# Attention and gated experts on one core: other places for the small products of the period, and the first batch's first score tiles straight from SBUF

## The reference

```python
x = x + attention(layernorm(x), w_qkv, w_out, b_out)      # 16 heads of width 8
x = x + experts(layernorm(x), router_w, router_b, w1, w3, w2)   # 4 experts, the best 2 per token
# attention weights: s = (q k^T) / sqrt(8); t = s - max(s); stablemax3(t) / sum,
#   for t < 0: 1 / (1 - t (1 - t/2 (1 - t/3)))
# expert: (silu(x w1) * (x w3)) w2, weighted by the two normalised gates, all in float32
```

## Time and profile before

| | us |
|---|---|
| median of 3 runs (lowest, highest) | 1129.02 (1128.45, 1129.56) |
| the profiled execution | 1130.74 |
| its span, first to last instruction | 1129.0 |

### The profile page before, as it was taken

One profiled execution on the slowest core, in us unless ns is written; L12 is line 12 of the kernel. 1 busy time (PEld: TensorE's weight loads), 2 busy tenths in 40 slices (PEclk: granted clock), 3 DMA queues, 4 the chain that ended last, 5 costly groups with the idle time before them and its releaser, 6 DMA issues.

```text
span 1129.0 us, 29283 instructions
## 1 busy us (share of the span) xinstructions
PE 1104.0 (98%) x9968; PEld 936.7 (83%) x9968; DVE 980.8 (87%) x1789; ACT 1004.1 (89%) x1034; POOL 750.7 (66%) x999
## 2 busy tenths in 40 slices
PE   5889999999999999999999999999999999999998
PEld 4768888888888888888888888888888888888888
DVE  4878999999989999999899999999989899998844
ACT  0699999999999999999999999999999999999982
POOL 5346667776766777676687776677767668776530
PEclk8999999999999999999999999999999999999999
DMA  4534333333332233433323343223333322333100
GB/s 119 176 114 151 107 96 94 100 121 122 119 103 91 83 120 119 127 113 97 92 89 121 122 126 107 90 94 101 121 122 117 104 89 84 119 123 124 30 6 11
DMA packets 130127, 117.49 MB, mean 104 GB/s; under 512 B 15492, under 2 KB 124708, under 8 KB 130084
## 3 DMA queue, kind: packets, MB, share of 16 engines
q1 hardware_dynamic: 127876, 113.78, 32.3%
q10 hardware_dynamic: 2208, 3.15, 0.8%
HBM read 94.70 MB, written 21.09 MB: 103 GB/s over the span
## 4 chain that ended last, share of the span: by engine, by line
PE 90%; ACT 4%; DVE 3%; DMA 1%; issue 1%; ACTq 0%; SPq 0%; DVEq 0%
PE banks L1275 33%; PE banks L1548 20%; PE sc L1361 11%; PE banks L1293 10%; PE sc L1531 4%; PE misc L1275 2%; ACT poly L741 2%; PE banks L1582 2%; ACT poly L746 1%; PE misc L1408 1%; PE misc L1426 1%; PE misc L1386 1%; PE banks L1531 1%; PE sc L1275 1%; DVE mx L968 1%
## 5 line engine op out<-in xcount | busy, mean ns | idle before, releaser
L462 POOL TENSOR_TENSOR hid<-hid,gate_all 128x512 f32<-128x512 f32 x240 | 379.2, 1643 | 155.9 <-DMA gate_all<-gate_scratch 139.8
L883 DVE SCALAR_TENSOR_TENSOR poly<-w_sq,sc 128x1024 f32<-128x1024 f32 x252 | 303.7, 1216 | 37.6 <-ACT w_sq L637 37.5
L1275 PE MATMUL banks<-xn_hi,w_hi 128*128 128x256 f32 x976 | 289.3, 296 | 0.2
L1275 PE MATMUL banks<-xn_lo,w_hi 128*128 128x256 f32 x976 | 275.4, 282 | 0.0
L1275 PE MATMUL banks<-xn_hi,w_lo 128*128 128x256 f32 x976 | 274.2, 281 | 0.0
L637 ACT ACTIVATE w_sq<-sc 128x1024 f32<-128x1024 f32 x252 | 255.5, 1029 | 7.3 <-PE sc L1361 3.5
L741 ACT ACTIVATE poly<-poly,two 128x2048 f32<-128x2048 f32 x128 | 252.1, 1991 | 0.4
L1548 PE MATMUL banks<-w_sb,hid 128*128 128x128 f32 x1920 | 246.1, 281 | 0.2 <-POOL hid L462 0.2
L968 DVE TENSOR_REDUCE mx<-sc 128x4 f32<-128x1024 f32 x192 | 229.8, 1213 | 11.5 <-PE sc L1531 10.4
L1548 PEld LDWEIGHTS banks<-w_sb,hid 128*128 128x128 f32 x1920 | 223.3, 191 | 16.4 <-POOL hid L462 0.5
L746 ACT ACTIVATE poly<-poly 128x2048 f32<-128x2048 f32 x128 | 236.8, 1896 | 0.0
(11 more groups left out here) (186 smaller groups left out, 1372.5 us busy)
## 6 DMA issues: line engine op xcount, KB each, us to landing
qk_scratch<-qk_split SPq DMA_DIRECT2D x32, 512.0 KB, 3.1
k_tile<-qk_scratch SPq DMA_DIRECT2D x128, 128.0 KB, 2.5
q_pad<-qk_scratch SPq DMA_DIRECT2D x256, 64.0 KB
q_tile<-qk_scratch SPq DMA_DIRECT2D x124, 128.0 KB, 2.5
k_stack<-qk_scratch SPq DMA_DIRECT2D x124, 128.0 KB
gate_all<-gate_scratch SPq DMA_DIRECT2D x30, 512.0 KB, 4.4
x_in<-in_L_attn_x_dram SPq DMA_DIRECT2D x32, 128.0 KB, 2.1
x_res<-in_L_attn_x_dram SPq DMA_DIRECT2D x32, 128.0 KB, 2.2
```

Source lines behind the costliest of these rows:

```text
L462: nc.gpsimd.tensor_tensor(h, h, by_token.unsqueeze(1).to_broadcast([128, 2, C, 128]), ALU.mult).then_inc(gated, 1)
L883: nc.vector.scalar_tensor_tensor(poly[:, u, :], w_sq[:, u % 2, :], 3.0, distance_buf(n, u), ALU.add, ALU.mult).then_inc(poly_ok, 1)
L1275: last = nc.tensor.matmul(dst, lhs[a], rhs[b], start=(k == 0), stop=(k == len(terms) - 1))
```

## The change

Five small pieces move in the settled periods, on PE and ACT, and the first batch's score tiles of groups 0 and 1 are copied from `qk_split` in SBUF rather than read back from DRAM. In the first case the code is written in another order; `attention_T` and `output_projection` become functions of the block, and ACT's copy `attention_T_copied` is called from the second half.

The diff, cut to its core:

```diff
@@ SP, first half
+                    if isinstance(i, int) and n == 0:
+                        sp.wait_ge(first_tiled[2], TILED)
+                    if isinstance(i, int) and n == -1:
+                        for r, part in enumerate((1, 3, 1, 3)):
+                            sp.dma_start(tile_group(k_tile, r, 0), group_part(part, 0)).then_inc(first_tiled[0], 16)
                     sp.dma_start(scratch.rearrange("a p t -> p a t"), ...
...
+                    if isinstance(i, int) and n == -1:
+                        for r, part in enumerate((1, 3, 1, 3)):
+                            sp.dma_start(tile_group(k_tile, r, 1), group_part(part, 1)).then_inc(first_tiled[1], 16)
                     sp.wait_ge(qk_stored, stored_qk)
                     after(sp, s_full, scored)
                     for r, part in enumerate((1, 3, 1, 3)):
+                        if isinstance(i, int) and n == -1:
+                            sp.dma_start(tile_rows(k_tile, r)[:, 2:G, :],
+                                         tile_part(part)[:, 2:G, :]).then_inc(first_tiled[2], 16)
+                            continue
@@ ACT, first half
                 if isinstance(i, int) and n == -1:
+                    act.wait_ge(qk_ok, 1)
+                    for g in range(2):
+                        for r, part in enumerate((0, 0, 2, 2)):
+                            nc.scalar.dma_start(tile_group(q_tile, r, g), group_part(part, g)).then_inc(first_tiled[g], 16)
                     act.wait_ge(qk_stored, 16)
                     for r, part in enumerate((0, 0, 2, 2)):
-                        nc.scalar.dma_start(tile_rows(q_tile, r), tile_part(part)).then_inc(tiled, 16)
+                        nc.scalar.dma_start(tile_rows(q_tile, r)[:, 2:G, :],
+                                            tile_part(part)[:, 2:G, :]).then_inc(first_tiled[2], 16)
@@ ACT, settled periods
                     square(6)
-                    attention_T_copied()
                     silu(6)
@@ ACT, second half
+                if settled(n):
+                    attention_T_copied(i, off)
                 if has(i, off):
                     log_of(0)
@@ PE, first half
                 if settled(n):
-                    values()
                     distance(0)
                     distance(1)
+                    values()
                     weighted_values(i, off - 1, 3)
...
@@ PE, scores of batch m
+                    if isinstance(i, int) and m == 0:
+                        pe.wait_ge(first_tiled[min(g, 2)], TILED)
@@ PE, second half
                     score(0)
                     down(0, 0)
+                    output_projection(i, off)
                     down(0, 1)
```

More of the change, by code:

```diff
@@ L205, in attention_then_experts_kernel @@
         tiled = sem("tiled")
+        first_tiled = [sem(f"first_tiled{i}") for i in range(3)]
         m_stacked = [sem(f"m_stacked{i}") for i in range(2)]
@@ L311, in tile_rows, with tile_group, group_part @@
             return tile[r::TERMS, :, :].bitcast(F32)
+        def tile_group(tile, r, g):
+            return tile[r::TERMS, g, :].bitcast(F32)
+        def group_part(part, g):
+            return qk_split[TILE * g:TILE * (g + 1), part // 2, S * (part % 2):S * (part % 2 + 1)].bitcast(F32)
         def tile_part(part):
@@ L477, in first_half @@
                     after(pool, qk_stored, 16 * m)
+                    if isinstance(i, int) and m == 1:
+                        pool.wait_ge(first_tiled[0], TILED)
+                        pool.wait_ge(first_tiled[1], TILED)
                     nc.gpsimd.tensor_tensor(qk_split[:, 0, :], qk[:], zero[:].to_broadcast([128, 2 * S]),
@@ L625, in _, with attention_T_copied @@
         def _(act):
+            def attention_T_copied(i, off):
+                m = no(i, off) - 1
+                act.wait_ge(attnT_full, m + 1)
+                after(act, res_full, m)
+                nc.scalar.copy(attn_T[:], misc[:, 0:S]).then_inc(attnT_ok, 1)
             def first_half(i, off):
@@ L669, in values_T_copied @@
                     nc.scalar.copy(o_T[:], pv).then_inc(o_ok, 1)
[L671 to L675, removed]
                 early = isinstance(i, int) and n == 1
@@ L1363, in distances, with attention_T, output_projection @@
                 last.then_inc(w_full, 1)
+            def attention_T(i, off):
+                n = no(i, off)
+                if not has(i, off - 1):
+                    return
+                m = n - 1
+                pe.wait_ge(attn_ok, m + 1)
+                for c in range(C):
+                    last = nc.tensor.transpose(misc[:, c * 128:(c + 1) * 128], attn[:, c, :], ident[:])
+                last.then_inc(attnT_full, 1)
+            def output_projection(i, off):
+                n = no(i, off)
+                if not has(i, off - 1):
+                    return
+                m = n - 1
+                pe.wait_ge(attnT_ok, m + 1)
+                for c in range(C):
+                    last = nc.tensor.matmul(misc[:, c * D:(c + 1) * D], attn_T[:, c * 128:(c + 1) * 128],
+                                            proj_T[:, 3, :], start=True, stop=True)
+                last.then_inc(res_full, 1)
             def first_half(i, off):
@@ L1440, in first_half @@
                     up_a_unit(i, off - 2, 3)
+                    values_T()
                     distance(4)
-                    values_T()
                     up_a_unit(i, off - 2, 4)
+                    up_b_unit(i, off - 2, 3)
                     distance(5)
-                    up_b_unit(i, off - 2, 3)
                     up_b_unit(i, off - 2, 4)
@@ L1448, in first_half @@
                     distance(6)
-                    attention_T()
                     up_a_unit(i, off - 2, 6)
@@ L1455, in first_half @@
                     up_b_unit(i, off - 2, 7)
-                    output_projection()
+                    attention_T(i, off)
                     return
@@ L1518, in scores @@
                     m, par = n + 1, (off + 1) % 2
+                    if isinstance(i, int) and m == 0:
+                        pe.wait_ge(first_tiled[min(g, 2)], TILED)
                     if g == 0:
                         after(pe, poly_ok, U * m)
-                        pe.wait_ge(tiled, TILED * (m + 1))
+                        after(pe, tiled, TILED * m)
                     else:
```

4 lines of the change are left out of this document (2 added, 2 removed).

## The result

The changed kernel takes 1134.52 us (median of 5 runs, 1134.28 to 1134.75) against 1128.96 before (1128.44 to 1129.56): ratio 1.0049, 95% interval 1.0038 to 1.0059, slower by 5.6 us. The forecast was 1128.4 with a range up to 1131.5. Its profiled execution took 1134.52, span 1132.8.

The account below looks back on a forecast made before the run. PE, 98% busy, was taken as the bound, and at the start a chain through SP, ACT and PE. Start -2.0 and periods +0.05 x 28 = +1.4 gave -0.6 us: 1128.4 us median, range 1124.5 to 1131.5.

Parts of the forecast that it names:

- First batch, -2.0: Program start: direct score tiles bring the first square from 38.92 to 36.9, behind w1's load and cast; -2.0 us.
- distance(4), distance(5), -0.22: Settled periods, PE: later places remove both late-release delays of 0.11; -0.22 us a period.
- up_a_unit(4), +0.05: Settled periods, PE: this unit now waits for silu(3), a delay formerly covered by distance(4); +0.05 us a period.
- attention_T, +0.22: Settled periods, PE: behind up_b_unit(7) nothing hides it, unlike in the wait for silu(5); +0.22 us a period.
- Output projection, 0: Settled periods: between the down products it costs PE 0.44 as before, with no wait for its operand; 0.
- values, 0: Settled periods, PE: same cost in both places; distance(0) taken not to wait for the maxima's DMA; 0, at most 0.17.
- Times 28: Settled periods: the sum of +0.05 us a period counted 28 times, giving +1.4 us.
- The waits go altogether: Rival, settled periods: PE's wait for silu(5) shrinks to nothing, 4.8 us won, 1122.2 with the start; chance 0.17.
- The maxima's DMA did take the place of a wait: Rival, settled periods: distance(0) waits for this DMA each period, 0.15 us times 28, 4.2 us, giving 1132.6; chance 0.12.
- The start gives nothing: Rival, first batch: stacked[0] lands at 29.4 or PE's clock falls; 0.5 of the gain left, 1129.9; chance 0.22.
- the late end of 29.4: First batch: latest landing that lets w1 be issued, if each 32 KB copy costs its full overhead; 27.9 was taken.

Follow-up runs that it names:

- e2: The kernel before with only the change's moves in the settled periods, first batch as before: 1133.67 us, ratio 1.0038.
- e6: The kernel before with values_T ahead of distance(4), up_b_unit(3) ahead of distance(5) and up_a_unit(5) ahead of up_b_unit(4): 1120.20 us, ratio 0.9922.
- e8: The kernel before with only the output projection moved behind the first down product: 1130.29 us, ratio 1.0008.
- e1: The kernel before with only the change's first-batch edits, direct score tiles of groups 0 and 1: 1130.22 us, ratio 1.0008.
- e15: The changed kernel with attention_T and ACT's copy of it back in their old places: 1128.13 us, ratio 0.9991 against the kernel before.
- e3: The kernel before with only values_T moved ahead of distance(4) and up_b_unit(3) ahead of distance(5): 1124.97 us, ratio 0.9963.
- e11: The kernel before with direct score tiles of group 0 alone, SP's four copies behind the store to DRAM: 1128.07 us, ratio 0.9990.
- e9: The kernel before with ACT issuing w3's load only once w1 has landed, ahead of the cast: 1131.76 us, ratio 1.0015.
- e14: The kernel before with w3's load placed behind the cast of w1 in ACT's program: 1131.41 us, ratio 1.0014.

## Why the prediction was wrong, by its own steps

From the first square to the last `values_T` the changed kernel takes 1093.67 - 38.90 = 1054.77, before 1089.87 - 38.92 = 1050.95: +3.8 where the sum had +1.4. The rest is the start.

- **First batch, -2.0: the step that failed.** Three parts of it. (1) The path. The sum ends with w1 and the cast and takes their end, 36.9, off a first square of 38.92. But in the earlier trace rows themselves the cast is over at 34.25 + 1.90 = 36.15, and ACT then waits 2.77 for `distance(0)`. In the changed kernel too the cast was over in time (36.05) and `distance(0)` at 38.16 wasn't. I had it at "about 35", with 3.09 for the maxima's DMA; that DMA was issued at 33.41, 1.5 later than this asks for, and took 4.75, since w1 and w3 were in its way. (2) The base. In the six other executions with the old start (e2 to e6, e8) the first square comes at 36.9 to 37.7, middle 37.2, and the maxima's DMA is issued at 32.1 to 33.4; the earlier trace rows show 38.92 and 35.09. PE was late there: its scores began at 22.55 (21.2 to 21.6 in the six) and ran on at the lower clock for longer, as the stretches and the last score group show, before and then e2 (columns as in the earlier trace rows; that w1 took 7.14 to the cast, 5.3 to 5.7 in the six, set nothing, since the cast was over first):

```profile
28.00:34.00 6.00, 5.96 (x37) 4.80 (x36) 5.20 (x5) 0.37 (x1) 1.30 (x1) 0.62 0.86 315
30.76 0.80 PE L1531 MATMUL sc<-k_tile,q_tile 32*128 32x256 f32 x8
```

```profile
28.00:34.00 6.00, 5.39 (x44) 4.49 (x43) 5.42 (x7) 1.58 (x2) 1.26 (x1) 0.93 0.87 304
29.21 0.51 PE L1539 MATMUL sc<-k_tile,q_tile 32*128 32x256 f32 x8
```

I counted a gain against this late start, and then deducted the 1.7 by which that execution stood above the median once more: the two are the same lateness. (3) The issue. w1 was issued at 28.61, 0.7 later than my 27.9, and some 1.6 later than in the six (26.6 to 27.3). Against 37.2 the start lost 1.7 (0.9 in e1) instead of gaining 2.0. With +3.8 this makes 5.5, the measured 5.6.
- **distance(4), distance(5), -0.22, and up_a_unit(4), +0.05: nearly right**, -0.146 for -0.17. The delay of `distance(5)` went. That of `distance(4)` did not: from 199.67 to 200.22 it takes 0.55, because it follows `values_T` now. Before, it was an up unit that followed `values_T` and took 0.81 up to the next group where 0.72 is usual (means over the periods). I had missed that term on both sides.
- **attention_T, +0.22: right**, 0.227 by e15. This was worked out and outweighs both delays, as the prediction said.
- **Output projection, 0, and values, 0: mis-sized**, 0.026 each. `distance(0)` wasn't released by the maxima's DMA in any settled period. With the projection moved, the first two `weighted_values` take 1.805 instead of 1.774 up to the next group, in e8 as in the changed kernel; that DVE's work, queued behind the later sum, is why, is argued and not shown.
- **Times 28.** The 27 periods between the two marks took 3.3 more where 27 x 0.05 = 1.35 was counted, 0.07 a period more by the two terms above and `distance(4)`. (PE's table names the bare wait 30 times, once in each settled period, so 28 was two short: 0.1 us.) The rest, 0.5, is outside them: the stretches between `values_T` at the two ends changed by -0.49 (28.08 to 27.59) and by +1.11 in the last three, of which some 0.5 each way is the earlier place of that mark itself, and that up to the first mark by -0.10.
- **The rivals.** "The waits go altogether" was wrong for this change, but its size was there to be had: e3 and e6. The maxima's DMA did take the place of a wait, in the first batch and not in the periods. "The start gives nothing" was the nearest; it should have held the chance that the start loses, since the issues ahead of the store can only delay. Its clock did fall, to 0.50, the 1.2 GHz level, after PE had been busy for only 2.72 us of the 5 from 22 to 27 (stretch of the changed kernel, columns as in the earlier trace rows):

```profile
30.00:34.00 4.00, 3.91 (x14) 2.70 (x15) 1.15 (x3) 0.03 (x1) 1.94 (x1) 0.50 0.93 351
```

This cost nothing at the first square: PE was through with its spare products and waited 1.50 for the maxima's DMA, and e15, which issued that DMA 1.35 earlier, has `distance(0)` at the same 9.55 behind w1.

The Trainium skill, "DMA: Bandwidth & Descriptors", "Rules for kernel authors", says to coalesce small transfers, and by it I gave the late end of 29.4. The measured issue, 28.61, lies between that and my 27.9. e11, with half the copies and none ahead of the store, is about 2 us faster than e1; it agrees with the rule, but changes the order too, so it doesn't show the number of copies to be the cause. The Trainium skill, on the same page under "Queues, rings and completion order", says that a DMA engine takes turns between the queues that have work for it, packet by packet. By that alone the maxima's 32 KB would not wait for 2 MB of another queue. The trace disagrees: 9.38 to 9.75 behind w1 in twelve executions, 6.52 against 3.21 in e9 and e14, and no packet of the small DMA for 2.1 us in the changed kernel and 3.8 in e15. The Trainium skill also says there that the write which signals completion lands only after earlier writes of that DMA engine, across its queues. That can be no more than a part here, since the packets themselves come late; from the stretch in which they moved to `distance(0)` it is 1.6 in the changed kernel (36.6 to 38.16) and 0.7 in e14 (34.8 to 35.54). What keeps the packets back stays open.

## What to carry to other kernels

A small product that stands where the engine waits anyway is free; before moving it, ask what will stand in that wait next, and if nothing does, move work into it, as e6 does, until the next releaser (here DVE, 0.2 behind) is reached. A one-time stretch with DMAs in it varies by more than the change under study (36.9 to 38.9 here), so its durations must not come from one execution, and the distance of that execution from the median may be this very stretch. A small DMA on which a chain waits belongs well ahead of bulk loads, also when they are on another queue. Before a gain is counted at a point where two chains meet, read which of them ends last there, in the trace of the kernel before too.

## What the runs showed of the hardware that was not expected

- A 32 KB DMA issued 0.26 behind a 1 MB load on another queue took 6.52 us to its reader, issued 0.52 ahead of it 3.21. Where it was behind two such loads, its packets didn't move until theirs were nearly through (none in the 2.1 us behind its issue, against 413 of the other queue).
- A DMA from ACT's queue was issued at the start of the cast that stands ahead of it in the program (32.85 and 32.84), not behind its 1.90.
- These copies and reads cost their issuing engine 0.6 to 0.7 us each, the same for 32 KB and 128 KB; the four ahead of the store made it 2.5 later in e1 (14.12 against 11.61).
- `distance(4)` and the up unit take 0.09 longer directly behind the four 128-column transposes; the cost goes to whatever comes next.
